# Gated cross-attention block: one column in front of each row of the scan for the carried r

## The reference, cut to what matters

```python
r = decay * r + kt * vt                 # kt = vt = ctx[t], so r = decay*r + ctx[t]**2
retained = (qt * r).reshape(B, D)       # qt = layernorm(x)[t]
inp = retained @ Wi.T + bi
gate = sigmoid(inp @ Wg.T + bg)
blended = gate * state + (1.0 - gate) * inp
state = tanh(blended @ A.T + inp @ Bm.T)
out = state @ Wo.T + bo
```

## Time and profile before

| | |
|---|---|
| median of three runs | 340.19 us |
| the profiled execution, its own time | 339.52 us |
| its span (first to last instruction) | 337.3 us |
| mean granted TensorE clock | 0.973 of full |
| TensorE busy (page, part 1) | 311.4 us, 92% of the span |
| VectorE busy | 292.8 us, 87% |
| ScalarE busy | 221.1 us, 66% |
| GpSimd busy | 72.7 us, 22% |
| one body in the middle (start to start) | about 18.46 us |

### The profile page before, as it was taken

How to read it: one execution, slowest core, us unless ns; L and a number is a source line. 1 busy time by engine, 2 the same in 40 slices (tenths; PEclk the granted TensorE clock), 3 DMA queues, 4 the chain that set the end, 5 groups by cost and what they waited for, 6 DMA issues and landing times.

```text
span 337.3 us, 9934 instructions
## 1 busy us (share of the span) xinstructions
PE 311.4 (92%) x3727; PEld 279.4 (83%) x3727; DVE 292.8 (87%) x868; ACT 221.1 (66%) x505; POOL 72.7 (22%) x107
## 2 busy tenths in 40 slices
PE   7867887999999999999999999999999999999985
PEld 5656766889898998989898989899898989897764
DVE  5887898999898989989898989899898989868653
ACT  3664546676759586766767585867677675757653
POOL 2021123132131222131311312221313112121220
PEclk9995697999999999999999999999999999999999
DMA  7920413217151434324161615243241415150530
GB/s 269 385 95 1 96 31 68 62 33 157 31 118 73 79 113 62 117 41 124 33 154 31 132 55 93 93 62 124 40 115 41 83 31 94 33 95 0 95 63 33
DMA packets 19239, 29.16 MB, mean 86 GB/s; under 512 B 1808, under 2 KB 10000, under 8 KB 18960
## 3 DMA queue, kind: packets, MB, share of 16 engines
q0 software_dynamic: 8704, 8.39, 17.5%
q1 hardware_dynamic: 10080, 19.93, 17.2%
q10 hardware_dynamic: 432, 0.53, 0.5%
HBM read 16.26 MB, written 4.19 MB: 61 GB/s over the span
## 4 chain that ended last, share of the span: by engine, by line
PE 72%; DVE 11%; ACT 11%; issue 2%; DMA 2%; SPq 1%; POOL 0%; DVEq 0%
PE pre_ps L804 13%; PE hid_ps L890 12%; PE y_ps L902 11%; PE ret_ps L804 9%; PE inp_ps L804 7%; PE pre_ps L845 7%; PE att_ps L863 5%; PE pre_ps L851 4%; ACT inp L359 3%; DVE inp_lo L536 3%; ACT inp_hi L363 3%; DMA w_raw<-w_in 2%; PE att_ps L872 2%; ACT state L404 2%; PE ret_ps L815 2%
## 5 line engine op out<-in xcount | busy, mean ns | idle before, releaser
L404 ACT ACTIVATE state<-pre_ps,sc 128x64 f32<-128x64 f32 x128 | 40.0, 312 | 80.4 <-PE pre_ps L851 79.8
L394 ACT ACTIVATE hid<-hid_ps,b_s 128x256 f32<-128x256 f32 x128 | 53.5, 470 | 14.4 <-PE hid_ps L890 12.6
L890 PE MATMUL hid_ps<-xt_hi,w_q 128*128 128x256 f16 x256 | 59.2, 272 | 1.4 <-DVE xt_lo L606 1.0
L902 PE MATMUL y_ps<-w_q,h_hi 128*128 128x256 bf16 x256 | 59.3, 273 | 0.3 <-DVE h_lo L613 0.3
L890 PE MATMUL hid_ps<-xt_lo,w_q 128*128 128x256 f16 x256 | 59.2, 272 | 0.0
L902 PE MATMUL y_ps<-w_q,h_lo 128*128 128x256 bf16 x256 | 59.1, 272 | 0.0
L613 DVE TENSOR_TENSOR h_lo<-hid,h_hi 128x512 f16<-128x512 f32 x64 | 44.0, 687 | 8.4 <-ACT h_hi L400 6.8
L845 PE MATMUL pre_ps<-m_hi,a_hi 128*128 128x32 f16 x508 | 42.7, 179 | 7.0 <-DVE m_hi L564 7.0
L845 PEld LDWEIGHTS pre_ps<-m_hi,a_hi 128*128 128x128 f16 x508 | 34.7, 97 | 15.0 <-DVE m_hi L564 12.3
L845 PE MATMUL pre_ps<-m_hi,a_lo 128*128 128x32 f16 x508 | 41.6, 177 | 0.0
L400 ACT CAST h_hi<-hid 128x512 f16<-128x512 f32 x64 | 39.6, 618 | 2.0
(11 more groups left out here) (128 smaller groups left out, 877.0 us busy)
## 6 DMA issues: line engine op xcount, KB each, us to landing
x_norm<-x_in SPq DMA_DIRECT2D x16, 256.0 KB, 2.8
cx<-ctx_in SPq DMA_DIRECT2D x16, 256.0 KB, 3.0
x_res<-x_in SPq DMA_DIRECT2D x16, 256.0 KB, 2.6
x_res<-bo_g POOLq DMA_DIRECT2D x16, 256.0 KB, 4.8
x<-b_g POOLq DMA_DIRECT2D x16, 256.0 KB, 3.9
y_out<-y SPq DMA_DIRECT2D x16, 256.0 KB, 2.0
w_raw<-w_in SPq DMA_DIRECT2D x2, 1024.0 KB, 9.3
wsq<-wsq_in SPq DMA_DIRECT2D x3, 256.0 KB, 6.1
```

The source lines that it names most:

```text
L394: last = nc.scalar.activation(hid[:, p % 2, u, :], hid_ps[p % 2][:, u * N:(u + 1) * N], ACT.Relu, bias=b1_s[:, 2 * p + u:2 * p + u + 1], s ...
L404: nc.scalar.activation(state[:, q[1] % 2, :, step_cols(j)], pre_ps[q[1] % 2][:, :].rearrange("p (k n) -> p k n", k=K)[:, :, step_cols(j)], ...
L890: last = nc.tensor.matmul(hid_ps[p % 2][:, u * N:(u + 1) * N], w1_q[:, k, cut], v[:, par, k, :], start=n == 0, stop=n == len(terms) - 1)
L902: last = nc.tensor.matmul(y_ps[:, t * D:(t + 1) * D], h[:, f, t * P:(t + 1) * P], w2_q[:, f, :], start=f == 0 and t == 0 and h is h_hi, st ...
```

## The change

The tiles cx2, keep and r get nine columns a row instead of eight. Column 0 of a cx2 row now holds the last r of the chunk before, with keep 0 there, so that the scan starts each row with it and multiplies it by decay in column 1. ScalarE copies it there (`carry`), ahead of `square` in slot 5. GpSimd sets the column to zero once at the start. The two scalar_tensor_tensor of `scan` are gone; `scan` waits for the copy's semaphore instead. The scan goes over 2 x 32 x 9 = 576 columns instead of 512. `retain` reads columns 1 to 8, so that its stride between batches is 36 bytes instead of 32. `square` writes 64 pieces of eight columns with one left out between them.

```diff
-        cx2 = sb("cx2", [P, K, B, T])
-        keep = sb("keep", [P, K, B, T])
-        r = sb("r", [P, K, B, T])
+        cx2 = sb("cx2", [P, K, B, T + 1])
+        keep = sb("keep", [P, K, B, T + 1])
+        r = sb("r", [P, K, B, T + 1])
...
+            nc.gpsimd.memset(cx2[:, :, :, 0], 0.0)
             nc.gpsimd.memset(state[:, 1, :, N - B:N], 0.0).then_inc(const_set, 1)
...
+            def carry(q):
+                act.wait_ge(r_set, upto(q))
+                nc.scalar.copy(cx2[:, :, :, 0], r[:, :, :, T]).then_inc(r_carried, 1)
+
             def square(q):
...
-                nc.scalar.activation(cx2[:, :, :, :], cx[:, q[1] % 2, :, :, :], ACT.Square).then_inc(squared, 1)
+                nc.scalar.activation(cx2[:, :, :, 1:T + 1], cx[:, q[1] % 2, :, :, :], ACT.Square).then_inc(squared, 1)
...
             scaled_high(a_hi, WA, S_A)
+            carry((0, 0))
             square((0, 1))
...
                         if norm:
+                            carry(project)
                             square(norm)
...
                 if exists(plus(q, -1)):
-                    for k in range(K):
-                        last = nc.vector.scalar_tensor_tensor(
-                            out=cx2[:, k, :, 0], in0=r[:, k, :, T - 1], scalar=cols[:, C_DECAY + k:C_DECAY + k + 1],
-                            in1=cx2[:, k, :, 0], op0=ALU.mult, op1=ALU.add)
-                    last.then_inc(r_first, 1)
-                    dve.wait_ge(r_first, upto(plus(q, -1)))
+                    dve.wait_ge(r_carried, upto(plus(q, -1)))
                 nc.vector.tensor_tensor_scan(r[:, :, :, :].rearrange("p k b t -> p (k b t)"),
...
-                                        r[:, :, :, :].rearrange("p k b t -> p k t b"), ALU.mult).then_inc(ret_set, 1)
+                                        r[:, :, :, 1:T + 1].rearrange("p k b t -> p k t b"), ALU.mult).then_inc(ret_set, 1)
...
-                last = nc.vector.tensor_scalar(keep[:, k, :, 1:T], keep[:, k, :, 1:T],
+                last = nc.vector.tensor_scalar(keep[:, k, :, 1:T + 1], keep[:, k, :, 1:T + 1],
```

More of the change, by code:

```diff
@@ L146, in build @@
         stats1, mean1, vare1, rstd1, xh1_set = (sem(n) for n in ("stats1", "mean1", "vare1", "rstd1", "xh1_set"))
-        squared, r_first, r_set = sem("squared"), sem("r_first"), sem("r_set")
+        squared, r_carried, r_set = sem("squared"), sem("r_carried"), sem("r_set")
         xh1_t = sem("xh1_t")
```

## The result

| | before | changed |
|---|---|---|
| median | 339.86 us (339.10 to 340.24, four runs) | 335.60 us (334.68 to 336.17, four runs) |
| ratio | | 0.9875, interval 0.9842 to 0.9908 |
| the profiled execution, its own time | 339.52 us | 336.17 us |
| its span | 337.3 us | 334.0 us |
| one body in the middle | 18.47 us | 18.23 us |

The changed kernel is 4.3 us faster, as the prediction's sum had it, and 0.1 us from the 335.7 us that it said.

A forecast was written before the change was run, and what follows sets the result against it. TensorE's chain was taken as the bound, held at step 7 by VectorE's scan. 14 bodies x 0.29 = 4.1 us plus 0.2 us made 4.3 us off, so 335.7 us (335.0 to 337.0; wider range 334.2 to 339.3).

The forecast's parts named there:

- The stall at step 7: TensorE waiting behind VectorE's scan for m_hi and m_lo: 0.75 us against 0.44 unheld, 0.31 us lost a body.
- TensorE's other wait in the middle: TensorE's wait for inp_lo, 0.46 us in each body, which the change was said not to touch.
- The small instructions: Two VectorE instructions ahead of the scan; removing them, with the scan's wait for the second, saves 0.49 us.
- The copy: ScalarE's 64-column copy ahead of the square: taken at 0.27 us, starting the square 0.15 us later (0.08 to 0.32).
- the wait ahead of the scan: VectorE idle until ScalarE's square ends, the copy's only part to show: 0.06 us.
- Retain: VectorE instruction in slot 1, reading at 36 instead of 32 bytes: no change taken; bounds -0.34 to +1.09 us.
- B: No change: step 7's gain is lost at another wait, through slower retain or square; 339.5 to 340.3 us, chance 0.12.
- C: Slower: the 36-byte pitch makes retain 0.55 us dearer and TensorE waits; 343.5 us, chance 0.07.
- D: Retain gets cheaper by all of 0.34 us, worth 1.0 us more; 334.7 us, chance 0.07.
- A: Part of the gain: copy nearer 0.44 us, or square or retain 0.1 to 0.2 us dearer; 337.9 us, chance 0.18.
- The limit of 0.31 us: What TensorE loses at step 7 in a body; the forecast gain was 0.29 us, the smaller of 0.31 and 0.29 + 0.02.
- The scan of body 0, slot 1: This scan on the chain would gain 0.355 us; half, 0.2 us, taken because 0.48 us of unexplained issue follows.

The follow-up runs named there:

- the early copy: Changed kernel with ScalarE's copy alone moved from slot 5 to the end of slot 4: 333.56 us, ratio 0.9817, body 18.13 us.
- no carry: Kernel before without the two small instructions or any carry, r starting from zero in each chunk: 334.04 us, ratio 0.9822, body 18.13 us.

## Why the prediction was right

*Where the change pays:* right. The stall at step 7 is where it was gained (0.75 to 0.52 us), and TensorE's other wait in the middle did not change.

*The terms of a body.* The small instructions: from rest to scan it was 1.10 us (0.61 and their 0.49) and is 0.73 (0.61 and a wait of 0.12), so they left in full. The longer scan: 1358 ns where 1.36 us was worked out, and the slope also gives the half scans (754 ns). The copy was taken at 0.27 us and took 0.318; it moved the square by 0.20 us where I had 0.15. The square took 652 ns, 15 more. So the wait ahead of the scan was 0.12 us instead of 0.06, and a body gained 0.49 - 0.135 - 0.12 = 0.235 us instead of 0.29. The copy made twice shows that this wait is paid in full (0.20 us more from rest to scan, 0.21 a body); the early copy gave back 0.10 of the 0.12 us, up to the cap.

*Retain:* 1079 ns against 1081, so 36 bytes cost what 32 do. Rivals B (in that form), C and D fall with this number alone; A was right in its kind (the copy dearer than taken), and about a third as large as it supposed.

*The limit of 0.31 us:* right in size; with no carry at all a body gained 0.33 us.

*The sum.* 14 bodies of 0.24 are 3.3 us, and the two profiled executions differ by 3.35. The medians differ by 4.3 and 5.0. That agreement is in part luck. In this pair 2.5 us lie between the slot 6 scans of bodies 0 and 13, which is 13 distances; 0.7 lie between body 0's own two scans (15.75 to 15.03 us), 0.25 ahead of them, and 0.2 are lost behind the last scan. So the time agrees with the forecast better than its terms do. The bodies are 0.7 us short of the forecast, and the medians have 1 us or more that the bodies don't. Where that comes from stays open; in the profiled executions it is not in bodies 3 to 13. Its size goes with the granted clock. At a mean of 0.975 or less, 23 executions of the kernel before have a median of 340.18 us and two of the changed kernel took 336.17 and 336.10, some 4.0 us less; at 0.985 or more, 15 have a median of 339.32 us and three took 334.28, 334.28 and 334.10, some 5.1 us less.

*The scan of body 0, slot 1.* I had half of 0.355 us, for fear of the 0.48 us of issue behind it. In both profiles of the changed kernel that gap is gone (the first has the scan at 22.58 and retain at 24.03, where they had been at 22.83 and 24.60), so nothing absorbed this part, and the gap went besides. The gap may not belong to the kernel before at all: its single trace has 0.54 us of idle there, while all twelve others have about 0.1, the one with no carry and the old layout too (scan at 22.47 for 1.22 us, retain at 23.79). What made it stays open, and its loss isn't shown to be a gain of the change.

## What to carry to other kernels

When two engines' lists run side by side between two meeting points, compare the distance of the same starts in a held and an unheld step. Here that gave the most that a cut on the late engine brought (0.31 us forecast, 0.33 found), before the cut was priced. Work moved to an engine with a low busy share still has to be placed: here the copy put a wait of 0.12 us ahead of the scan from slot 5, and none from slot 4. When cuts on either engine alone bring little or nothing, try them together; here it was 0.15 and 0.00 us a body alone and 0.39 together.

## What the runs showed of the hardware

- tensor_tensor_scan in f32 took 686, 754, 1224 and 1358 ns for 256, 288, 512 and 576 columns, a line of 148 ns + 2.10 ns a column.
- Reading r with 32 or with 36 bytes between columns costs retain the same (1081 and 1079 ns). That is 0.34 us over y, another instruction of 512 columns with contiguous operands (742 ns); that the distance between columns makes this difference is argued, not shown.
- A copy of 64 columns, 36 bytes apart on both sides, took 318 ns on ScalarE, but only 0.20 us from its start to that of the next; on VectorE 0.30 us, and 0.33 us to the scan that waited for it.
- The granted TensorE clock from 22 to 60 us was 0.78 in the one profile of the changed kernel and 0.87 in the other, and in the middle 1.00 in both. From the slot 6 scan of body 0 to that of body 1 it was 18.88 us in the one and 17.53 us in the other, and from there to body 2's 18.79 and 20.31. Single bodies at the head of the run thus differ by over 1 us between executions of one kernel, and their sum here by 0.17 us, while the bodies from 3 to 13 agree within 0.01 us on average (18.23 and 18.23).
